# 64-wide attention: an own order for the first batch's rounds, and expert blocks without a drain

## The reference, cut to what matters

```python
x = x + attention(layernorm(x), ctx, ctx, L0...)    # 16 heads of 16
x = x + expert_choice_ffn(layernorm(x), L0_ffn...)  # 16 experts, each takes 64 tokens of every 512
x = x + attention64(layernorm(x), ctx, ctx, L1...)  # 16 heads of 64
x = x + top2_experts(layernorm(x), L1_ffn...)       # 8 experts, 2 per token
x = x + context_attention(layernorm(x), ctx)        # no projections
...                                                 # quantised FFN, attention, block-quantised linear

def attention64(h, c):            # b: batch, h: head, d: 64
    Q, K, V = h @ Wq.T + bq, c @ Wk.T + bk, c @ Wv.T + bv
    attn = softmax(Q K^T / 8)     # per head, 256 x 256
    return (attn V) @ Wo.T
```

## Time and profile before

| | us |
|---|---|
| median of 3 runs | 1683.46 (1682.42 to 1688.7) |
| profiled execution, its own time | 1683.53 |
| its span | 1681.7 |
| expert-choice block, last instruction of POOL ends | 587.9 |
| 64-wide attention, first instruction | 593.25 |
| its first scores | 611.7 |
| its end | 1013.9 |
| top-2 block, last scatter ends | 1215.8 |
| block behind it, first instruction | 1222.6 |

### The profile page before, as it was taken

One profiled execution on the slowest core, in us unless ns is written; L12 is line 12 of the kernel. 1 busy time (PEld: TensorE's weight loads), 2 busy tenths in 40 slices (PEclk: granted clock), 3 DMA queues, 4 the chain that ended last, 5 costly groups with the idle time before them and its releaser, 6 DMA issues. The chain is left out here.

```text
span 1681.7 us, 29336 instructions
## 1 busy us (share of the span) xinstructions
PE 1415.6 (84%) x9650; PEld 1138.7 (68%) x9650; DVE 1078.5 (64%) x2487; ACT 836.1 (50%) x1944; POOL 488.6 (29%) x428
## 2 busy tenths in 40 slices
PE   5899974999999749999999995699856897888885
PEld 4666542888888647888888873599744786555553
DVE  4677643666666537777787765644366753688886
ACT  2466541544544437666677764255423543455551
POOL 2112011577777610000000004255412311134343
PEclk8899876999999979999999997699978997799997
DMA  4322124456556345544554434122173002222110
GB/s 144 122 87 84 50 101 163 113 140 163 134 136 164 60 126 141 127 115 114 133 131 104 108 120 133 34 77 77 60 227 105 1 0 62 74 78 74 60 52 26
DMA packets 140109, 168.91 MB, mean 100 GB/s; under 512 B 20136, under 2 KB 131880, under 8 KB 137448
## 3 DMA queue, kind: packets, MB, share of 16 engines
q1 hardware_dynamic: 115000, 131.42, 26.7%
q0 software_dynamic: 16032, 27.01, 7.5%
q10 hardware_dynamic: 8976, 9.17, 1.8%
HBM read 75.66 MB, written 24.12 MB: 59 GB/s over the span
## 5 line engine op out<-in xcount | busy, mean ns | idle before, releaser
L1131 ACT ACTIVATE a_probT<-a_t 128x512 f32<-128x512 f32 x256 | 151.6, 602 | 164.6 <-PE a_t L860 138.5
L941 DVE TENSOR_REDUCE a_nmax<-a_s 128x2 f32<-128x512 f32 x256 | 170.9, 685 | 92.2 <-PE a_s L856 92.0
L63 POOL TENSOR_TENSOR a_rstd<-a_veps,minus_half 128x2 f32<-128x2 f32 x32 | 23.2, 724 | 507.1 <-DVE a_veps L57 507.1
L856 PE MATMUL a_s<-a_ka,a_qa 48*128 48x256 f32 x512 | 123.2, 342 | 44.8 <-DVE a_nmax L941 21.2
L856 PEld LDWEIGHTS a_s<-a_ka,a_qa 48*128 48x128 f32 x512 | 78.6, 202 | 105.3 <-issue 61.4
L441 DVE TENSOR_REDUCE a_nmax<-a_score 128x2 f32<-128x512 f32 x128 | 88.0, 687 | 86.7 <-PE a_score L334 86.6
L536 ACT ACTIVATE a_prob<-a_score,a_nmax 128x256 f32<-128x256 f32 x256 | 120.3, 481 | 34.4 <-DVE a_nmax L441 34.3
L1665 POOL DMA_INDIRECT x_rows<-f_hn,f_scatter_row x60 | 129.9, 2164 | 16.4 <-issue 16.4
L860 PE MATMUL a_t<-a_qa,a_ka 50*128 50x256 f32 x512 | 123.2, 339 | 2.2 <-DMA a_qa<-a_m_lo 1.2
L1608 ACT ACTIVATE f_gate<-f_gate 128x512 f32<-128x512 f32 x64 | 38.3, 599 | 129.0 <-PE f_gate L1411 111.0
L1521 DVE TENSOR_TENSOR f_y<-f_gate,f_value 128x512 f32<-128x512 f32 x64 | 44.0, 688 | 80.4 <-PE f_value L1411 78.4
(11 more groups left out here) (385 smaller groups left out, 4414.3 us busy)
## 6 DMA issues: line engine op xcount, KB each, us to landing
area_odd<-in_L_experts SPq DMA_DIRECT2D x15, 1536.0 KB, 6.8
a_k_hi<-a_k_fresh_hi SPq DMA_DIRECT2D x128, 128.0 KB, 2.4
a_ctxT<-in_ctxT SPq DMA_DIRECT2D x64, 128.0 KB, 2.6
a_ka<-a_k_hi SPq DMA_DIRECT2D x128, 64.0 KB, 2.6
a_k_lo<-a_k_fresh_lo SPq DMA_DIRECT2D x64, 128.0 KB, 2.4
a_q<-a_q_fresh_hi SPq DMA_DIRECT2D x64, 128.0 KB, 2.4
a_q<-a_q_fresh_lo SPq DMA_DIRECT2D x64, 128.0 KB, 2.4
a_qa<-a_q_hi SPq DMA_DIRECT2D x120, 64.0 KB, 2.6
```

Of the source, the lines that this page charges most:

```text
L856: last_s = nc.tensor.matmul(ps_s[i][:, half, :], qa[rows, u % RING, j, half * P:(half + 1) * P], ka[rows, u % RING, j, :], start=True, sto ...
L941: nc.vector.tensor_reduce(nmax[:, u % 2, :, i * PPU + j], ps_s[i][:, :, :], AX.X, ALU.max, negate=True).then_inc(sem["nmax"], 1)
L1131: nc.scalar.activation(probT[:, t % NPT, i, :, :], ps_t[i][:, :, :], ACT.Exp).then_inc(sem["exp"], 1)
```

## The change

1. The first batch gets an order of its own: `early` becomes k 0, hT, v 0, q 0, v 1, k 1, and `FIRST_STEP` keeps q 1, k 2, q 2, k 3, q 3, v 2, v 3. The banks follow this order for the first batch (`order`, `bank`).
2. ACT rounds the context before it writes zeros; the first zeros follow the context, the second ones follow hT. `zeros` counts to 2. DVE makes the context's low part before it applies the norm.
3. The high parts of q 0 are copied by ACT (`place_first_queries`, two DMAs on its queue), the low parts by SP (`copies[1:]`). SP no longer waits for the zeros, and places k 1 before the first step's list.
4. POOL computes rstd of batch 1 before it rounds Wo.
5. Both expert blocks are built with `no_gpsimd_drain=True`. `scatter_row` gets memory that no later stage reuses.

```diff
--- before.py
+++ after.py
@@ -142,8 +142,9 @@
             ("k", 3): NU + 1, ("q", 3): NU + 2, ("v", 2): NU + LAG, ("v", 3): NU + LAG + 1}
     rounds = list(STEP)
 
-    early = ["hT", ("k", 0), ("q", 0)]
-    FIRST_STEP = {("k", 1): 0, ("q", 1): 0, ("v", 0): 1, ("k", 2): 1, ("v", 1): 2, ("q", 2): 2, ("k", 3): 3, ("q", 3): 3, ("v", 2): 4, ("v", 3): 4}
+    early = [("k", 0), "hT", ("v", 0), ("q", 0), ("v", 1), ("k", 1)]
+    FIRST_STEP = {("q", 1): 0, ("k", 2): 1, ("q", 2): 2, ("k", 3): 3, ("q", 3): 3, ("v", 2): 4, ("v", 3): 4}
+    first_rounds = early + list(FIRST_STEP)
     OUT_STEP = LAG + 2
     CTX_STEP = LAG + 3
     OUT = len(rounds) % NPB
@@ -163,7 +164,7 @@
     def rounds_at(s, b, more, delay=0):
 
         if first(b):
-            own = [name for name in rounds if name in FIRST_STEP and FIRST_STEP[name] + delay == s]
+            own = [name for name in first_rounds if name in FIRST_STEP and FIRST_STEP[name] + delay == s]
         else:
             own = [name for name in rounds if STEP[name] + delay == NU + s]
         return [(name, b) for name in own] + [(name, b + 1) for name in rounds if more and STEP[name] + delay == s]
@@ -203,9 +204,17 @@
         weights = {"k": (w.WkT, w.Wk_hi, w.Wk_lo), "q": (w.WqT, w.Wq_hi, w.Wq_lo), "v": (w.WvT, w.Wv_hi, w.Wv_lo)}
         proj = (sem["proj0"], sem["proj1"])
 
+        def order(f):
+
+            return first_rounds if first(f) else rounds
+
+        def bank(f, name):
+
+            return ps_p[order(f).index(name) % NPB]
+
         def projected(f, name):
 
-            r = rounds.index(name)
+            r = order(f).index(name)
             return proj[r % NPB], f * PER[r % NPB] + r // NPB + 1
 
         def placed(f, what, i):
@@ -242,7 +251,7 @@
                 sp.dma_start(chip.x[:, s * GT:(s + 1) * GT, :], chip.x_rows.rearrange("(t p) d -> p t d", p=P)[:, s * GT:(s + 1) * GT, :]).then_inc(chip.x_back[s], 16)
             context(1)
 
-            def place(f, what, i):
+            def place(f, what, i, parts=("hi", "lo")):
 
                 sp.wait_ge(sem[what + "_lo"], f * NCH + (i + 1) * CPR)
                 hi, lo = fresh[what]
@@ -250,7 +259,7 @@
                     own, other = rows(half)
                     heads = slice(2 * CPR * i + half, 2 * CPR * (i + 1), 2)
                     copies = [(k_hi, own, hi), (k_hi, other, hi), (k_lo, own, lo)] if what == "k" else [(q2, own, hi), (q2, other, lo)]
-                    for to, at, part in copies:
+                    for to, at, part in copies if len(parts) == 2 else copies[1:]:
                         sp.dma_start(to[at, heads, :].bitcast(F32), part[own, :, :].bitcast(F32)).then_inc(placed(f, what, i)[0], 16)
 
             def places(b, more, part=None):
@@ -263,9 +272,9 @@
                     if s == CTX_STEP and b + 2 < B:
                         context(b + 2)
 
-            sp.wait_ge(sem["zeros"], 1)
-            for what in "kq":
-                place(0, what, 0)
+            place(0, "k", 0)
+            place(0, "q", 0, parts=("lo",))
+            place(0, "k", 1)
             places(0, True)
             n = prefetch.beside(sp, sem["wload"])
             for b in range(1, B - 1):
@@ -280,11 +289,11 @@
         def _(pe):
             def claim(f, name):
 
-                r = rounds.index(name)
+                r = order(f).index(name)
                 if r >= NPB:
-                    pe.wait_ge(*consumed(f, rounds[r - NPB]))
+                    pe.wait_ge(*consumed(f, order(f)[r - NPB]))
                 elif not first(f):
-                    last_of_bank = rounds[r::NPB][-1]
+                    last_of_bank = order(f - 1)[r::NPB][-1]
                     pe.wait_ge(*consumed(f - 1, last_of_bank))
                     if r == OUT:
                         after(pe, sem["xadd"], f - 1)
@@ -388,7 +397,7 @@
 
             for name in early:
                 front(0, name)
-            pe.wait_ge(sem["zeros"], 1)
+            pe.wait_ge(sem["zeros"], 2)
             batch(0, True)
             with pe.Fori(1, B - 1) as b:
                 batch(b, True)
...
@@ -485,8 +494,8 @@
 
             dve.wait_ge(chip.x_back[0], 16)
             norm_stats(nc, dve, chip.x, sem, nb, 0, TB, 0)
+            context_low(0)
             norm_apply(nc, dve, chip.x, sem, nb, 0, TB, 0, hn, sem["hn"])
-            context_low(0)
             for name in early:
                 read_round(0, name)
             batch(0, True)
...
@@ -565,14 +574,29 @@
                     if more and s == CTX_STEP:
                         context_high(b + 1)
 
-            for h in range(2):
+            def zeros(h):
+
                 own, other = rows(h)
                 finite = chip.ident[other, :].unsqueeze(1).unsqueeze(1).to_broadcast([HD, NCH, KC, P])
-                last = nc.scalar.activation(k_lo[other, :, :].rearrange("p (c h) (a b) -> p c h a b", h=2, b=P)[:, :, h, :, :], finite, ACT.Copy, scale=0.0)
-            last.then_inc(sem["zeros"], 1)
+                nc.scalar.activation(k_lo[other, :, :].rearrange("p (c h) (a b) -> p c h a b", h=2, b=P)[:, :, h, :, :], finite, ACT.Copy,
+                                     scale=0.0).then_inc(sem["zeros"], 1)
+
+            def place_first_queries():
+
+                act.wait_ge(sem["q_hi"], CPR)
+                for half in range(2):
+                    own, other = rows(half)
+                    act.dma_start(q2[own, slice(half, 2 * CPR, 2), :].bitcast(F32),
+                                  fresh["q"][0][own, :, :].bitcast(F32)).then_inc(placed(0, "q", 0)[0], 16)
+
             context_high(0)
+            zeros(0)
             for name in early:
                 read_round(0, name)
+                if name == "hT":
+                    zeros(1)
+                if name == ("q", 0):
+                    place_first_queries()
             batch(0, True)
             with act.Fori(1, B - 1) as b:
                 batch(b, True)
@@ -588,8 +612,8 @@
             chip.sems.clear_last_stage(nc)
 
             norm_rstd(nc, pool, chip, sem, nb, TB, 0)
+            norm_rstd(nc, pool, chip, sem, nb, TB, 1)
             nc.gpsimd.tensor_copy(w.Wo_hi, w.WoT).then_inc(sem["Wo_hi"], 1)
-            norm_rstd(nc, pool, chip, sem, nb, TB, 1)
             pool.wait_ge(sem["Wo_hi"], 1)
             nc.gpsimd.tensor_tensor(w.Wo_lo, w.WoT, w.Wo_hi.bitcast(F32), ALU.subtract).then_inc(sem["Wo_lo"], 1)
             with pool.Fori(2, B) as f:
@@ -1308,7 +1332,7 @@
         token = sb("token", [P, SLOTS, E], U32)
         next_token = sb("next_token", [P, 2, SLOTS], U32)
         gather_row = sb("gather_row", [P, 2, SLOTS], U32)
-        scatter_row = sb("scatter_row", [P, 2, SLOTS], U32)
+        scatter_row = chip.scatter_row
 
         rows = hn[:, 0:2 * SLOTS, :].rearrange("p (q s) d -> p q s d", q=2)
         z = hn[:, 2 * SLOTS:4 * SLOTS, :].rearrange("p (q s) d -> p q s d", q=2)
@@ -1336,7 +1360,7 @@
         def three(a_hi, a_lo, b_hi, b_lo):
             return (a_hi, b_hi), (a_hi, b_lo), (a_lo, b_hi)
 
-        block = ctx.enter_context(nc.Block())
+        block = ctx.enter_context(nc.Block(no_gpsimd_drain=True))
 
         @block.sync
         def _(sp):
@@ -2790,6 +2814,7 @@
         chip.y_back = [nc.alloc_semaphore(name=f"y_back{b}") for b in range(B)]
         chip.ident = sb("ident", [P, P])
         chip.minus_half = sb("minus_half", [P, TILES])
+        chip.scatter_row = sb("scatter_row", [P, 2, GROUPS], U32)
         area_even, even_parts = area("area_even", 9728)
         area_odd, odd_parts = area("area_odd", 12288 + 500)
         chip.landed = [nc.alloc_semaphore(name=f"landed{s}") for s in range(GROUPS)]
```

16 lines of the change are left out of this document (8 added, 8 removed).

## The result

| | before | after |
|---|---|---|
| median beside each other, us | 1685.99 (1680.98 to 1699.39, 20 runs) | 1677.76 (1669.69 to 1686.73, 20 runs) |
| ratio to before | | 0.995, 95% interval 0.9935 to 0.9966 |
| profiled execution: span in us, mean granted clock of PE | 1681.7, 0.918 | 1680.5, 0.915 |

A forecast was written before the change was run, and what follows sets the result against it. PE leads overall (84% busy), but two POOL drains and PE's waits in the attention's first batch bound the changed places; 5.15 + 6.5 + 5.3 = 16.95 us off 1683.5 gave 1666.6, range 1662 to 1676 (own range 1663 to 1671).

The forecast's parts named there:

- Edit 1: Expert-choice block's end: without POOL's drain the attention starts 5.15 us earlier; a drain of about 5 us moves to POOL's clear.
- The own place of scatter_row costs nothing: Memory for scatter_row in the expert blocks: giving it a place of its own was put at no cost.
- Edit 2: Attention's front: context ahead of zeros and a new order of rounds; k 0 starts on PE at T+4.3, bounds T+1.5 to T+5.1.
- T: Start of the 64-wide attention, its first SP load; 593.25 us before, forecast 588.1.
- full clock: PE at granted clock 1.00 from v 0 on: first scores T+17.5, gain of 7.5 us at the sixth scores; half clock 5.3.
- Edit 3: Attention's first batch: ACT takes two q copies; first scores T+17.5 to T+19.7, first k 1 copy T+18.0 or T+20.2, before T+26.3.
- Edit 4: POOL's new order in the attention: Wo's rounding overlaps VectorE's normalising; price 1.3 us, bounds 0 and 6.4.
- Edits 2 to 4 together: Attention's new front: gain of 6.5 us at the sixth scores, bounds 3 to 8.8, staying to the end.
- Edit 5: Top-2 block's end: without POOL's drain the next fetch starts at 1217.35 instead of 1222.64; gain 5.3 us, bounds 3.0 and 5.4.
- the signs of being wrong: In the attention: hT starting later than T+9, or the sixth scores coming later than T+43.
- Rival (b): POOL's drain starts anew in the next block, as long as the 13.1 us one; total gain 6.0, time 1677.5; chance 0.08.
- rival (a): Attention's new order gives almost nothing: half clock, POOL holding VectorE longer, SP's queue setting the pace; 1673 us; chance 0.20.

The follow-up runs named there:

- e13: The kernel before with only scatter_row moved to a place of its own ahead of the weight areas, drains kept; median 1688.48 us, ratio 1.0007.
- e2: The changed kernel with POOL's drain put back in both expert blocks; median 1687.41 us, ratio 0.9995.
- e5: e3 with one reload of x ahead of the expert-choice block's end instead of two; 1665.59 us beside 1683.37 for the kernel before.
- e9: e3 with SP placing all four q 0 copies again, none on ACT; 1673.6 us beside 1683.99 for the kernel before.
- e3: The changed kernel with POOL rounding Wo after the applied norm of batch 0, ahead of rstd of batch 1; median 1671.59 us, ratio 0.9925.
- e4: The changed kernel with Wo's low part made by four POOL subtractions instead of one; 1671.43 us beside 1685.64 for the kernel before.
- e7: The changed kernel with POOL's old order, Wo's CAST ahead of rstd of batch 1; 1682.86 us beside 1683.37 for the kernel before.

## Why the prediction was wrong, by its own steps

**Edit 1: right at its place, wrong in its cover.** Forecast 5.15; the gap behind the last scatter shrank by 5.16 us (5.33 to 0.17). The drain of 5 us that I expected at the clear took 0.10, so the step was right with less risk than I gave it. That the old drains ended 5.1 and 6.5 us after the last generation had told me they followed the scatters; I did not conclude that a drain in the next stage need not.

**"The own place of scatter_row costs nothing": wrong, about 3 us.** It is 2.8 in e13, 3.1 in e2, and 3.5 by the stage of after, which gained 1.7 us of edit 1's 5.16: over half of it was taken back. I had weighed this line as free because it adds no instruction.

**Edit 2: right with the drain kept, late without it.** k 0 came at T+6.0, not T+4.3, and outside my bounds of T+1.5 to T+5.1. With the drain kept (e2) it came at T+4.5, so the sum itself was right and the missing drain is what made it late: transfers that used to end under the drain's 5 us were still moving at T. The reload of x issued at 585.98 is one; leaving it out (e5) gave back 0.8 of the 1.5 us, and the rest stays open. The transfers issued in the first microseconds of the attention, from 585 to 597 us in after, then from 590 to 600 in before (KB each, median us from issue to landing):

```profile
x_tok<-x_rows SPq DMA_DIRECT2D x3, 512.0 KB, 4.1
a_ctxT<-in_ctxT SPq DMA_DIRECT2D x4, 128.0 KB, 3.5
```

```profile
x_tok<-x_rows SPq DMA_DIRECT2D x2, 512.0 KB, 4.5
a_ctxT<-in_ctxT SPq DMA_DIRECT2D x4, 128.0 KB, 2.4
```

The delay reached the end. PE's granted clock was 1.00 from T+9.4 to T+19.6, so the forecast to compare with is the one for full clock, first scores at T+17.5 and K, the first copy of k 1, at T+18.0. e2 came near it, with T+18.6 at both; after had T+20.5 at both. e2's sixth scores are 2.0 us ahead of after's.

**Edit 3: right in kind.** What moved was K, by 4.5 to 5.8 us, in front of the unchanged chain. The first scores moved too, 2.0 us later, to T+20.5, outside the forecast T+17.5 to T+19.7; in e2, with the context early, they stood at T+18.6. Its part on ACT was worth nothing (e9), which the prediction did not separate.

**Edit 4: the step that failed most.** Forecast 1.3 us within 0 to 6.4. From K to the sixth scores the forecast had 19.1 us without the overlap and 20.4 with it; e3 and e9 took 19.2 and 19.4, after 24.0. So edit 4 cost up to 4.8 us; against e5, which had a shorter fall of the clock there and took 20.2, 3.8. The mechanism was named rightly: the pair took 4.52 us against 0.62. The Trainium skill, SBUF — State Buffer, section "SBUF: two separate sides", has VectorE (in a mode that uses two ports, or with two inputs in SBUF against a GpSimd instruction that reads SBUF) and GpSimd take a shared port pair as an exclusive lock for the whole instruction. By this pair and e4's pieces the trace agrees with the lock; which mode VectorE was in, no row shows. The size was wrong for two reasons. The sum let the stall hit only q 2's low part, with k 2's copies on time at K+7.5 and SP busy until K+11.4. In the trace the pair stood in front of k 2's low part, the chain that paces all: K+12.1. POOL itself was through at K+10.3, near the K+9.8 of the sum; what was wrong is who waits behind it. And the stall's length was set by the order on VectorE at that moment; a shift of 2 us between the engines (e7) changes it by 1.9. I had chosen the value nearest the one row that showed an overlap, and the case for it rested on a time of arrival known to no better than 1 to 2 us.

**Edits 2 to 4 together** were put at 6.5, of which 1.3 was already taken off; the sixth scores moved by 0.6 (the mean 45.1 of before to 44.5) and the stage by nothing. Taken from the full-clock forecast of 7.5: 0.8 is the base, 45.9 in the one profile of before where three have a mean of 45.1; 2.5 lie ahead of K (T+20.5 for T+18.0), up to 2.0 of them by the late context (by e2; e3 and e9, whose context was as late, were 0.9 and 0.7 behind e2); and 3.6 behind K (24.0 for 20.4), by the stall and, for some 0.9, by the clock. e3 without the overlap gives 6.5 at the sixth scores and 7.3 in the stage, so the gain existed. That it stays once gained was nearly right: from the sixth scores to the stage's end there are 374.6 to 375.0 us before, 375.7 after, 373.8 in e2 and e3.

**Edit 5: right.** Forecast 5.3; the gap shrank by 5.23, the stage by 5.0.

**The account.** Forecast 16.95, by stage 5.15, 6.5 and 5.3. Measured by stage 1.7, -0.4 and 5.0: 3.5 us went at the expert choice, by the place of scatter_row, and 6.9 in the attention, by the stall, the late context and the base. These three stages leave 6.3, the five 6.8, inside the measured 5.7 to 11.0. Of the signs of being wrong that the prediction named, one came (sixth scores later than T+43); hT started at T+8.7, just short of the other. Rival (b) gives nearly the measured time, 1677.5, but its mechanism was absent (0.10 us at the clear); rival (a) came closest in kind, an order that gives nothing by POOL holding VectorE, and its 1673 lacks the cost of the place; nothing showed SP's queue as the pace (e9).

## What to carry to other kernels

When a wait at a stage's end goes, look for transfers that used to finish under it: here the next stage's first load was read 1.5 us later, 0.8 of it by a reload of x, and the stage became up to 3.9 us longer (e2 against after, one execution each). Before moving a long POOL instruction, list VectorE's SBUF-only instructions in the stretch where it will land and what is queued behind them; put it where VectorE works from PSUM or waits. And count an allocation as an edit of its own: one that adds no instruction cost about 3 us here, and putting it behind the weights instead of ahead of them gave this back.
